# Flamingo gated blocks, first expert layer: the blocks' pipeline started one loop step after the shared units

## The reference

```python
def _ffn(xn, rw, W1, W2):
    ms = jnp.mean(xn * xn, axis=-1, keepdims=True)
    h = xn * jax.lax.rsqrt(ms + RMS_EPS) * rw
    return jax.nn.silu(h @ W1) @ W2
...
gates = jax.nn.softmax(xf @ router_w, axis=-1)       # 1792 tokens, 14 experts
top_v, top_i = jax.lax.top_k(gates, TOP_K)           # 2 experts for each token
...
routed_out = jnp.einsum('end,ne->nd', routed, masked)
shared = jax.vmap(...)(rms_w_s, w1_s, w2_s).sum(0)   # 2 experts that take all tokens
return (routed_out + shared).reshape(B, T, D)
```

## Time and profile before

| | us |
|---|---|
| median of 3 runs | 930.98 |
| lowest and highest run | 930.15, 931.14 |
| span of the profiled execution | 930.4 |
| PE busy in it | 728.2 (78%) |
| DVE busy | 607.6 (65%) |
| ACT busy | 476.9 (51%) |
| POOL busy | 487.0 (52%) |

### The profile page before, as it was taken

The page is one execution under the profiler, slowest core; times in us unless marked ns, Lnnn a source line. Parts: engine busy times, 40 slices in busy tenths (PEclk is TensorE's granted clock), DMA queues, the critical chain, the costliest instruction groups (busy, mean ns, idle before and its releaser), DMA issues. The chain is left out here.

```text
span 930.4 us, 21111 instructions
## 1 busy us (share of the span) xinstructions
PE 728.2 (78%) x6870; PEld 545.1 (59%) x6903; DVE 607.6 (65%) x1448; ACT 476.9 (51%) x969; POOL 487.0 (52%) x608
## 2 busy tenths in 40 slices
PE   3878999999884999888888888587678368998830
PEld 2445666666663898776666666466577335665420
DVE  6665777777766799834444443777887256667766
ACT  3545666666563777623333331455564146776632
POOL 5797788797301478820000003777865517647455
PEclk9998999999996799989999997789988569999985
DMA  6344444432201478542222212496431113323233
GB/s 167 91 118 111 115 111 115 119 93 73 56 3 44 140 258 257 188 130 68 69 68 69 69 56 84 128 230 188 138 92 40 55 51 110 102 75 98 81 91 101
DMA packets 87664, 98.96 MB, mean 106 GB/s; under 512 B 17260, under 2 KB 77132, under 8 KB 87564
## 3 DMA queue, kind: packets, MB, share of 16 engines
q1 hardware_dynamic: 63468, 66.10, 24.0%
q0 software_dynamic: 16432, 24.66, 9.9%
q10 hardware_dynamic: 7664, 6.89, 2.6%
HBM read 61.03 MB, written 24.38 MB: 92 GB/s over the span
## 5 line engine op out<-in xcount | busy, mean ns | idle before, releaser
L783 DVE TENSOR_REDUCE a_mx<-ps 112x2 f32<-112x750 f32 x128 | 120.2, 939 | 51.4 <-PE ps L401 49.7
L673 POOL DMA_DIRECT2D a_stkK<-a_KS x248 | 119.2, 489 | 20.9 <-issue 14.9
L643 ACT ACTIVATE a_Pf<-ps 125x672 f32<-125x672 f32 x128 | 90.0, 729 | 14.1 <-PE ps L345 13.0
L1830 POOL MEMSET a_half<- 112x2 f32 x1 | 0.1, 94 | 169.7 <-POOLq L89 169.7
L51 PE MATMUL ps<-f_w2hi,f_hh 128*128 (+1 forms) x292 | 80.3, 275 | 4.1 <-issue 2.9
L1541 DVE CAST f_hh<-ps 128x512 bf16<-128x512 f32 x41 | 28.4, 693 | 83.9 <-PE ps L1281 83.9
L51 PE MATMUL ps<-f_w2hi,f_hl 128*128 (+1 forms) x292 | 80.2, 275 | 0.0
L51 PE MATMUL ps<-f_w2lo,f_hh 128*128 (+1 forms) x292 | 80.1, 274 | 0.0
L2455 POOL TENSOR_TENSOR f_rl<-f_rf,f_rh 128x512 bf16<-128x512 f32 x34 | 39.5, 1161 | 66.8 <-DVE f_rh L2523 65.4
L51 PE MATMUL ps<-f_w1hi,f_xgThi 128*128 x137 | 52.9, 386 | 21.9 <-DVE f_xgTlo L1534 15.4
L2399 ACT ACTIVATE f_rf<-ps,f_ln 128x128 f32<-128x128 f32 x136 | 54.5, 451 | 30.2 <-PE ps L2352 30.2
(11 more groups left out here) (397 smaller groups left out, 2339.2 us busy)
## 6 DMA issues: line engine op xcount, KB each, us to landing
a_raw<-F_w SPq DMA_DIRECT2D x22, 512.0 KB
f_xg<-f_xd SPq DMA_DIRECT2D x75, 128.0 KB
f_yd<-f_yo SPq DMA_DIRECT2D x75, 128.0 KB
f_raw<-F_w SPq DMA_DIRECT2D x14, 512.0 KB
a_ctxF<-ctxT SPq DMA_DIRECT2D x16, 375.0 KB
a_cR<-ctx SPq DMA_DIRECT2D x16, 375.0 KB
a_stkK<-a_KS POOLq DMA_DIRECT2D x248, 23.4 KB, 2.0
a_cT_first<-ctxT SPq DMA_DIRECT2D x14, 375.0 KB
```

The lines of the kernel that those rows point to most:

```text
L643: nc.scalar.activation(Pf[:, j % PB], psST[:C, j % 2, :, 0:SC * T], ACT.Exp, scale=DH ** -0.5).then_inc(exp_done, 1)
L673: pool.dma_start(stkK[SIDE * h + DH * a:SIDE * h + DH * (a + 1), w.slot, jj], KS[2 * DH * jj + DH * h:2 * DH * jj + DH * (h + 1), w.odd, p ...
L783: nc.vector.reduce_max(mx[:, n.odd, j // JJ, :, j % JJ], maxima_of(n, j)[:T, :, :S], AX).then_inc(mx_red, 1)
```

## The change

On all three engines the blocks' steps move one loop step later against the shared units: `up_rows` is now of unit s+1, `turn_hidden` of unit s, `down` of a block of unit s-1. A shared `down` now stands straight behind `up`, ahead of everything that belongs to blocks. `turned`, `x_high` and `x_low` of the first two blocks both fall into step 15; before, they stood in steps 13 and 14. The loop runs one step longer.

```diff
+        def turned_at(s):
+            return block_of(s + 2) if s >= 2 * SH - 1 else None
...
-                for s in range(-2, UNITS):
-                    t, n, h, m, d = block_of(s + 3), block_of(s + 2), block_of(s + 1), shared_of(s + 1), unit_of(s)
+                for s in range(-2, UNITS + 1):
+                    t, n, h, m, d = turned_at(s), block_of(s + 1), block_of(s), shared_of(s + 1), shared_of(s) or block_of(s - 1)
                     if m is not None:
                         up(m)
+                    if d is not None and d.shared is not None:
+                        down(d, None)
+                    if s == 2 * SH - 1:
+                        turned(block_of(s + 1))
                     if n is not None:
...
-                    if d is not None:
+                    if d is not None and d.shared is None:
                         down(d, expert.get(d.u))
-                    if s == UNITS - 2:
+                    if s == UNITS - 1:
...
-                for s in range(-2, UNITS):
-                    t, n, m, d = block_of(s + 3), block_of(s + 2), shared_of(s + 1), unit_of(s)
+                for s in range(-2, UNITS + 1):
+                    t, n, m, d = turned_at(s), block_of(s + 1), shared_of(s + 1), block_of(s - 1)
                     if m is not None:
                         silu(m)
                         high(m)
+                    if s == 2 * SH - 1:
+                        x_high(block_of(s + 1))
...
-                for s in range(-2, UNITS):
-                    t, m, d = block_of(s + 3), unit_of(s + 1), unit_of(s)
+                for s in range(-2, UNITS + 1):
+                    t, m, d = turned_at(s), shared_of(s + 1) or block_of(s), shared_of(s)
...
+                    if s == 2 * SH - 1:
+                        x_low(block_of(s + 1))
                     if m is not None:
                         halves(m)
```

More of the change, by code:

```diff
@@ L1411, in _ @@
                         x_high(t)
-                    if d is not None and d.shared is None:
+                    if d is not None:
                         out(d)
@@ L1567, in _ @@
                         x_low(t)
-                    if d is not None and d.shared is not None:
+                    if d is not None:
                         add_shared(d)
```

## The result

The changed kernel takes 934.23 us (median of 20 runs, 928.26 to 937.44), the kernel before 929.89 us (20 runs beside them, 924.09 to 933.87). The ratio is 1.0045, its 95% interval 1.003 to 1.006: slower by 4.3 us. The forecast was 928.5, faster.

The account below looks back on a forecast made before the run. PE was taken to be bound by order for 6.75 us, standing still for the first block's `xg`. From 930.98, 3.13 gained gives 927.85; plus 0.65 for the clock, 928.5, range 927.3 to 929.9.

Parts of the forecast that it names:

- 390.61: On PE, the issue end of unit 14's `up` in the kernel before, from which the changed order was costed.
- The start of the blocks: On PE, four short waits adding to 5.24 replace 8.37 lost; third `up_rows` at 409.71 instead of 412.84, 3.13 us earlier.
- The waits: PE's four stops: ahead of `down` of 15 0.68, first `up_rows` 1.18, second 1.44, third 1.94.
- the first: PE's wait ahead of `down` of unit 15: 0.68, with `halves` taking 0.1 to start and 1.08 to run.
- What costs nothing: Queue order on POOL and SP, later fourth load, `add_shared` in DVE's stops and the extra loop step: no added cost.
- just this as a sign against it: On SP, the first `xg` load issued much later than 395.4 would show the prediction wrong.
- The clock: At the blocks' start, one PE stretch at 1.2 GHz costs 1.3; hit in one execution of two, 0.65.
- B: At the blocks' start, one or two stretches at 1.2 GHz in nearly every execution: 929.15 or 930.45; chance 0.2.
- D: PE's clock falls at the first short stop and stays down until the fourth `up_rows`: 933.9, slower; chance 0.07.
- C: Gain lost before the barrier through later `xg` loads or `y` stores, or longer steps: about 931.0; chance 0.08.

Follow-up runs that it names:

- e1: The changed kernel with the rank products back ahead of the first shared `down`; 933.86 us, ratio 1.001 to the kernel before.
- e2: The kernel before with only the rank products moved behind the `down` of step 0; 941.6 us, ratio 1.01 to the kernel before.
- e3: e1 with `turned`, `x_high` and `x_low` of the first two blocks in step 14, ahead of `down` of 15; 931.1 us, ratio 0.9983 to the kernel before.
- e4: The changed kernel with `halves` of unit 1 ahead of `place()` on DVE; 937.76 us, ratio 1.0047 to the kernel before.
- e6: The changed kernel with the third load's split and `halves` of unit 1 both ahead of `place()` on DVE; one run, 930.8 us.
- e7: Repeat of e1 on the second chip; 926.33 us, ratio 0.9949 to the kernel before.
- e8: Repeat of e3 on the second chip; 923.8 us, ratio 0.9918 to the kernel before.
- e5: The kernel before, word for word, as a control on the second chip; 929.07 us, ratio 0.9996 to the kernel before.

## Why the prediction was wrong

**The step that failed** is the one that was not made: the change was costed only from the end of unit 14's `up` on, and 390.61 was taken over from the kernel before as if nothing ahead of it had moved. The diff's `down(d, None)` behind `up(m)` applies to all 16 shared units. In 15 of them nothing stands between the two; in step 0 the rank products do. The cost of it is 6.22; e1 takes it away, and e2 makes it from the old kernel. Against the forecast, 3.13 - 0.65 = 2.48 us faster, the markers are 5.98 off: 6.22 that was put at nothing, 0.41 less gained at the start of the blocks, and 0.65 for a clock that did not fall there. In the medians the gap to the forecast is 934.23 - 928.5 = 5.7, and the base had come out 1.1 lower besides (929.89 for 930.98).

**The start of the blocks** was right in mechanism and nearly in size: 2.72 gained, 3.13 forecast. The waits, start to start, forecast and measured: 0.68 and 1.03 (404.42 to 405.45), 1.18 and 1.18 (408.33 to 409.51; the row at 409.74 is the second matmul of its group), 1.44 and 1.46, 1.94 and 1.94. The term that was mis-sized is the first: `halves` of unit 15 started 0.45 after the end of `high` (403.85 to 404.30), not 0.1. It is 0.45 in all kernels that have the new order of the loops (e1, e3, e4, e6, e7, e8), and 0.10 in the kernel before, behind as long a stop of DVE (3.38 there, 3.35 here); so the length of the stop does not explain it, and what does stays open. The waits of PE in the earlier trace rows include one more long one that the prediction passed over, 9.1 for `xn`; it lies ahead of t0 and is 9.1 in both kernels.

**What costs nothing**: "POOL's and SP's queues keep their order up to the first `xg` load" is true, but an order says nothing of when it begins. The load went out at 400.98. The prediction had named just this as a sign against it. e6 shows that its lateness was not the cost, though.

**The clock** was placed wrongly. The four short stops did not lower it: 1.00 from 409 to 417, and the same in this part of e1, e3 (which has two of the stops), e4 and e6. B and D, which would have had it fall there, did not happen, and the 0.65 for it was not due. The Trainium skill, "TensorE: Matmul & The Clock Gate", section "A second HAM failure mode: psum-queue depth-cycling", tells of a kernel in which frequent short stops of PE made the clock go down and up; the start of the blocks here does not do so, with stops of 0.86, 1.24, 1.29 and 1.78 within 12 us and a clock of 1.00. It fell 73 and 50 us ahead of these stops, behind those of 3.84 and 2.19. C, a gain lost again before the barrier, did not happen either: the 2.72 is all there at 571.97 against 575.52.

The slower side was given 0.07, for D alone. The time came out there by a mechanism that no rival had.

## What to carry to other kernels

A line in a loop that is moved is moved in every iteration: list, for each engine, what now stands on its other side in each of them, one-off work above all, and not only at the place that the change is for. Where one engine waits in its queue for a result, the price of a delay is set by the work queued behind that wait; put what others need, and what frees the next load, ahead of it (e6). And where totals scatter by more than the effect, compare times between two markers inside the profile, with an unchanged kernel among them to show what they resolve (under 1 us here, where the intervals of the totals reach 1.4 us and more to either side).

## What the runs showed that was not expected

The clock does not follow the length of a stop alone. Behind stops of 3.84 and 3.85 it was low each time. At one place in the program, ahead of `down` of 5, it stayed at 1.00 behind 2.88 in the kernel before and 2.16 in e6 (and behind 2.29 to 2.89 in e1, e3, e5, e7 and e8), and fell behind 2.19 in the changed kernel, 2.93 in e4 and 2.02 in e2. The three that fell are those whose stop ends late, 33.4 to 34.6 after t0, where the others have 29.4 to 30.0. The three pairs of equal kernels agree here, so these traces give no sign that the fall is chance; what decides it is not shown.

Work behind the barrier, which no edit touches, took between 353.3 us (e7: 919.8 - 566.46) and 359.3 us (e3: 925.3 - 566.05), and the work ahead of t0 between 318.8 (e7: 318.58 + 0.26) and 328.4 (e8: 328.13 + 0.26). Either is about as much as the largest effect studied here, or more. It is why the changed kernel's profile has the shorter span: 353.5 behind the barrier, where the kernel before took 358.4, most of it the wait for `a_stkK`. The profiles with that wait have 356.2 to 359.3 behind the barrier, those without it 353.3 to 354.7.
